# A bidirectional selective scan: four of sixteen states injected by a diagonal matmul, conv outputs on ScalarE

## The chip, the cores and the metric

One NeuronCore of one Trainium2 chip runs the whole kernel in one launch. The metric is the device time of an execution in microseconds, the median of several. The work is fp32 in the part that is changed.

## The reference, cut to what matters

The network is a Mamba-like block (two directions) followed by an attention and mixture-of-experts block, with layer norms between. The change is in the first block, on a batch of 2 sequences of 2,048 tokens, 512 inner channels and 16 states:

```
xc = silu(causal_conv(x_in, conv_w) + conv_b)
dt, B, C = split(xc @ xp_w.T);  dt = softplus(dt @ dt_w.T + dt_b)
for t:  h = exp(dt_t * A) * h + (dt_t * x_t) * B_t     # for 512 channels x 16 states
        y_t = sum over states(h * C_t) + D * x_t
```

It is done once forward and once on the flipped sequence. In the rest of this text x in dt*x is xc.

## The kernel before, in words

The function scan_channels does the scan stage. Channels lie on the 128 partitions, in four groups m = 0 to 3 (DT). Time is cut into chunks of 512 steps. A unit f is one chunk of one direction of one batch; there are 2 x 4 x 2 = 16 units, forward and backward in turn (d = 0, 1). A unit has 64 scans, j = 4n + m for state n and channel group m. Each engine runs a list written out by hand, and semaphores join the lists.

For each scan j:

- ScalarE makes dA = exp(dt * A) for state n and group m (`decay`, L564). For each state it also scales the rows of the turned dt*x, where time lies on partitions, by B of that state (`spread_b`, L569): four activations of 128x512 into one of three dBxT buffers.
- TensorE turns the scaled rows back, four 128x128 transposes into one of three PSUM banks (`inject`, L820). It may fill a bank once the scan three back is done. It also adds the products of eight scans earlier into acc by transposes (`add`, L831). In a transpose the data and an identity are the two operands.
- VectorE runs the recurrence over 512 steps (`scan`, L728) from dA, the bank and the saved state, into hh.
- GpSimd copies the last column of hh to the saved state once per state (L514) and multiplies hh by C (L516). hh, hC and dA have two buffers, so scan n needs GpSimd's copy and products of n-2, and `decay` for n waits for the scan of n-2.

Among these stands the front of a coming unit. For unit f+1: `proj` (TensorE, before injects 7 to 10), `proj_out` (ScalarE), `turn_bc` before inject 15, `bt_out` (ScalarE, L538), `dt_of` (TensorE, L792, before injects 18, 21, 24, 27), each followed by `relu` (VectorE, L700, after that scan) and `dt_out` (ScalarE, L546), then one exponential over 2,048 columns (ScalarE, L551), an addition on GpSimd (L493), `softplus_low`, `softplus` and `times_x` (VectorE, L676, L682, L687, after states 8, 9, 10), `front_one_plus` and `front_log` (ScalarE, L556, L560), and four `turn_dtx` with `turned_out` (before inject 49, 51, 53, 55). For unit f+2: `conv` (TensorE, L769, four matmuls of 512 columns before injects 29, 33, 38, 43), each followed by `conv_out`, which adds the bias and copies to xc (VectorE, L694, after that scan), and a SiLU over all of xc (L526). `skip` (L838) multiplies xc by a diagonal of D, in four plain 128x128 matmuls, after injects 14, 16, 19 and 22.

All front results go through a single PSUM bank, fr: TensorE counts fr_mm as it fills it, the engine that empties it counts fr_out, and each filling waits for the emptying before. TensorE's instructions run in order, so an inject written behind a front matmul waits with it.

ScalarE's list in iteration n is: `spread_b(n+1)`, `middle(n)`, four `decay(n+1)`, `tail(n)`. middle(7) is the exponential, middle(8) `front_one_plus`, middle(9) `front_log`; tail(6) is dt_out(3), tail(12) the SiLU.

Of the kernel before, what the change touches and what calls it, by code (L numbers as in the profile page):

```python
# [16 lines left out]
ACT = mybir.ActivationFunctionType  # L17
# [7 lines left out]
P = 128  # L25
# [4 lines left out]
NS = 16  # L30
# [321 lines left out]
def scan_channels(nc, k, xin, crows, y, convw, convb, xpw, dtw, dtb, alog, dskip):  # L352

    with Stage(nc, "scan") as s:
# [5 lines left out]
        cb = s.sb("cb", [P, 2, DT])  # L360
# [21 lines left out]
        fr = s.ps("fr", [P, C])  # L382
# [19 lines left out]
        AT_DT, AT_NEXT, AT_TURN, AT_SKIP = (18, 21, 24, 27), (29, 33, 38, 43), (49, 51, 53, 55), (14, 16, 19, 22)  # L402

        LOOP = 2 * NC

        def bank(l, j):
            return (l * SUB + j) % (LOOP * SUB) % 3

        def turned_slot(l, n):
            return (l * NS + n) % (LOOP * NS) % 3  # L410

# [110 lines left out]
        def _(act):  # L522
# [25 lines left out]
            def front_exp(f, group):  # L548

                act.wait_ge(fr_out, group + 1)  # L550
                act.activation(ee[:, :, :], ee[:, :, :], ACT.Exp, scale=-1.0).then_inc(e_ok, 1)  # L551

            def front_one_plus(f):
                act.wait_ge(e_ok, f + 1)
                act.wait_ge(y_stored, f * 16 + 16)
                act.activation(uu[:, :, :], ee[:, :, :], ACT.Identity, bias=k["one"][:, :]).then_inc(u_ok, 1)  # L556
# [9 lines left out]

            def spread_b(d, l, n):
                for j in range(JT):
                    last = act.activation(dBxT[turned_slot(l, n)][:, j, :], dtxT[d][:, j, :], ACT.Copy,  # L569
                                          scale=bt[d][:, j, NS + n:NS + n + 1])  # L570
                last.then_inc(bd_ok, 1)
# [30 lines left out]
            def unit(b, c, d, f):  # L602
                o, g, first = 1 - d, f + 1, f * FR_ALL + FR_BEGIN

                def middle(n):
                    if n == 2:
                        for half in range(2):
                            evacuate(f, half)
                    if n == 3:
                        proj_out(g, first + FR_PROJ)  # L610
                    if n == 4:
                        bt_out(o, first + FR_BT)
                    if n in (5, 6):
                        dt_out(o, g, n - 4, first + FR_DT + n - 4)
                    if n == 7:
                        front_exp(g, first + FR_DT + 3)
                    if n == 8:
                        front_one_plus(g)
                    if n == 9:
                        front_log(g)  # L620

                def tail(n):
                    if n == 3:
                        store(f)
                    if n == 4:
                        dt_out(o, g, 0, first + FR_DT)
                    if n == 6:
                        dt_out(o, g, 3, first + FR_DT + 3)
                    if n == 12:
                        silu(d, f + 2, first + FR_NEXT + 3)  # L630

                for n in range(NS):
                    q = f * NS + n
                    dn, at = (d, n + 1) if n + 1 < NS else (o, 0)
                    if n + 1 == NS:
                        act.wait_ge(fr_out, first + FR_TURN + JT)
                    act.wait_ge(bx_mm, f * SUB + turned_free(2 * c + d, n + 1))
                    spread_b(dn, (2 * c + d) + (n + 1) // NS, at)
                    middle(n)
                    if n + 1 == NS:  # L640
                        act.wait_ge(dt_ok, g + 1)
                    for m in range(DT):
                        decay(dn, q + 1, at, m)
                    tail(n)
# [8 lines left out]
        def _(dve):  # L653
# [35 lines left out]
            def conv_out(d, f, m, group):  # L689
                if m == 0 and not (isinstance(f, int) and f < 2):  # L690
                    dve.wait_ge(skip_ok, f - 1)
                    dve.wait_ge(front_ok, f - 1)
                dve.wait_ge(fr_mm, group + 1)
                dve.tensor_scalar(xc[d][:, m, :], fr[:, :], cb[:, d, m:m + 1], None, ALU.add).then_inc(fr_out, 1)  # L694
# [36 lines left out]
            def unit(b, c, d, f):  # L731
                o, g = 1 - d, f + 1
                first = f * FR_ALL + FR_BEGIN
                dve.wait_ge(zeroed, b + 1)
                for n in range(NS):
                    for m in range(DT):
                        scan(d, 2 * c + d, f, n, m)
                        at = n * DT + m
                        if at in AT_DT:
                            i = AT_DT.index(at)  # L740
                            relu(o, g, i, first + FR_DT + i)
                        if at in AT_NEXT:
                            i = AT_NEXT.index(at)
                            conv_out(d, f + 2, i, first + FR_NEXT + i)
                        if at in AT_TURN:
                            i = AT_TURN.index(at)
                            turned_out(o, i, first + FR_TURN + i)
                    if n == 8:
                        softplus_low(o, g)
                    if n == 9:  # L750
                        softplus(o, g)
                    if n == 10:
                        times_x(o, g)
# [4 lines left out]
        def _(pe):  # L758
# [52 lines left out]
            for m in range(DT):  # L811
                conv(1, 14 + m, 1, m)

            def inject(l, f, j):
                n, m = j // DT, j % DT
                if m == 0:
                    pe.wait_ge(bd_ok, f * NS + n + 1)
                pe.wait_ge(h_ok, f * SUB + bank_free(l, j))
                for t in range(JT):
                    last = pe.transpose(bx[bank(l, j)][:, t * P:(t + 1) * P],  # L820
                                        dBxT[turned_slot(l, n)][:, t, m * P:(m + 1) * P],
                                        k["ident"][:, :])
                last.then_inc(bx_mm, 1)

            def add(f, a):
# [22 lines left out]
            def unit(b, c, d, f):  # L848
                o, g, first = 1 - d, f + 1, f * FR_ALL + FR_BEGIN
                for j in range(SUB):  # L850
                    if 7 <= j < 11:
                        proj(o, g, first + FR_PROJ, [j - 7])
                    if j == 15:
                        turn_bc(first + FR_BT)
                    if j in AT_DT:
                        m = AT_DT.index(j)
                        dt_of(o, m, first + FR_DT + m)
                    if j in AT_NEXT:
                        m = AT_NEXT.index(j)
                        conv(d, first + FR_NEXT + m, f + 2, m)  # L860
                    if j in AT_TURN:
                        t = AT_TURN.index(j)
                        turn_dtx(g, t, first + FR_TURN + t)
                    inject(2 * c + d, f, j)
                    for a in adds.get(j, []):
                        add(f, a)
                    if j in AT_SKIP:
                        skip(d, AT_SKIP.index(j))
# [1495 lines left out]
```

## Time and profile before

| what | value |
|---|---|
| median of 3 runs | 4084.34 us (4078.41 to 4086.13) |
| profiled execution | 4088.92 us |
| its span | 4087.3 us |
| TensorE busy | 3407.1 us, 83% |
| VectorE busy | 2777.7 us, 68% |
| ScalarE busy | 2461.5 us, 60% |
| GpSimd busy | 1913.2 us, 47% |
| 1,024 scans (L728) | 1243.5 us, 1263 ns each |
| 1,028 scaled-row activations (L569) | 655.4 us |
| 4,096 injecting transposes (L820) | 668.9 us |
| 72 conv_outs (L694) | 52.3 us |

The scan stage lasts from about 200 to 1,872 us of the span; the stages after it are not touched by the change. A busy time of TensorE counts pipelined matmuls, so a duration of one instruction is longer than the distance to the next start; the distance is the rate. The names PE, DVE, ACT and POOL in rows are TensorE, VectorE, ScalarE and GpSimd.

### The profile page before, as it was taken

The page shows a single profiled execution, that of the slowest core. Times are in us where ns is not written, and L with a number is a line of the kernel's source. Part 1 is how long each engine was busy: PE and PEld are TensorE (multiplying, and loading weights), DVE is VectorE, ACT ScalarE, POOL GpSimd, SP SyncE. Part 2 cuts the span into 40 slices and gives each one's busy share as a digit, 9 for nine tenths or more (in the row PEclk, how much of TensorE's full clock was granted, in tenths as well). Part 3 has the DMA queues.
Part 4 walks back from the last instruction along what each step waited for, and adds up shares of the span by engine and source line. Part 5 has one row for each costly group of instructions (what it writes and reads, how often), then busy time and mean ns, then how long its engine had stood idle before and what let it go on. Part 6 is the DMA issues. An engine that isn't in the chain of part 4 may idle for free. (4 is left out here: it accounts for less than half of the span.)

```text
span 4087.3 us, 69747 instructions
## 1 busy us (share of the span) xinstructions
PE 3407.1 (83%) x22940; PEld 2105.2 (52%) x22940; DVE 2777.7 (68%) x4397; ACT 2461.5 (60%) x3860; POOL 1913.2 (47%) x1734
## 2 busy tenths in 40 slices
PE   7568888888888888885876999999999996499994
PEld 3246666666666666664553333333333334366663
DVE  3259999999899999995764777777777753511113
ACT  3259999999999999993220555555555563122111
POOL 1049999999899999995431000000010002512222
PEclk9779999999999999998995999999999997599997
DMA  5633333333333333335634011011011014333323
GB/s 187 187 89 97 97 99 97 95 94 96 93 96 101 96 94 94 94 94 203 221 119 124 9 20 17 9 20 20 7 20 20 7 48 132 129 81 84 86 53 93
DMA packets 162170, 349.72 MB, mean 86 GB/s; under 512 B 20963, under 2 KB 74198, under 8 KB 147344
## 3 DMA queue, kind: packets, MB, share of 16 engines
q1 hardware_dynamic: 129904, 270.96, 23.9%
q0 software_dynamic: 20624, 43.82, 4.2%
q10 hardware_dynamic: 11280, 30.41, 2.0%
q8 instruction: 191, 3.13, 0.3%
q14 instruction: 171, 1.40, 0.1%
HBM read 245.04 MB, written 102.59 MB: 85 GB/s over the span
## 5 line engine op out<-in xcount | busy, mean ns | idle before, releaser
L516 POOL TENSOR_TENSOR scan_hC<-scan_hh,scan_cbc 128x512 f32<-128x512 f32 x1024 | 1376.4, 1374 | 84.5 <-DVE scan_hh L728 76.8
L728 DVE TENSOR_TENSOR_SCAN scan_hh<-scan_dA,scan_state,scan_bx 128x512 f32<-128x512 f32 x1024 | 1243.5, 1263 | 140.9 <-PE scan_bx L820 63.7
L1572 PE MATMUL attend_s<-attend_kt,attend_qt 32*128 32x512 f32 (+3 forms) x2560 | 803.3, 616 | 34.4 <-DMA attend_qt<-attend_zero 27.8
L820 PE MATMUL scan_bx<-kept_ident,scan_dBxT 128*128 128x128 f32 x4096 | 668.9, 289 | 151.0 <-DVE scan_hh L728 121.9
L564 ACT ACTIVATE scan_dA<-scan_dt,scan_an 128x512 f32<-128x512 f32 x1028 | 661.4, 712 | 30.5 <-DVE scan_hh L728 30.5
L820 PEld LDWEIGHTS scan_bx<-kept_ident,scan_dBxT 128*128 128x128 f32 x4096 | 487.7, 147 | 358.8 <-DVE scan_hh L728 243.2
L831 PE MATMUL scan_acc<-kept_ident,scan_hC 128*128 128x128 f32 x4128 | 646.4, 283 | 29.6 <-POOL scan_hC L516 22.6
L1593 PE MATMUL attend_s<-attend_qt,attend_kt 32*128 32x512 f32 (+3 forms) x2560 | 643.6, 588 | 16.3 <-POOL attend_pb L1449 13.9
L569 ACT ACTIVATE scan_dBxT<-scan_dtxT,scan_bt 128x512 f32<-128x512 f32 x1028 | 655.4, 711 | 0.2
L1483 DVE TENSOR_REDUCE attend_mx<-attend_s 128x1 f32<-128x512 f32 x768 | 494.9, 686 | 203.1 <-PE attend_s L1572 202.0
L1543 ACT ACTIVATE attend_pb<-attend_s 128x1024 f32<-128x1024 f32 x384 | 390.8, 1024 | 285.9 <-PE attend_s L1593 285.9
L1449 POOL TENSOR_SCALAR_AFFINE_SELECT attend_pb<-attend_pb 128x512 f32<-128x512 f32 x128 | 81.3, 636 | 990.6 <-ACT attend_pb L1552 990.6
L831 PEld LDWEIGHTS scan_acc<-kept_ident,scan_hC 128*128 128x128 f32 x4128 | 509.3, 148 | 43.5 <-POOL scan_hC L516 35.5
L1613 PE MATMUL attend_pv<-attend_pb,attend_vall 128*32 128x256 f32 (+1 forms) x4608 | 360.3, 388 | 31.7 <-POOL attend_pb L1449 30.8
L1572 PEld LDWEIGHTS attend_s<-attend_kt,attend_qt 32*128 32x128 f32 x2560 | 302.2, 196 | 118.8 <-DVE attend_mx L1483 44.2
L1593 PEld LDWEIGHTS attend_s<-attend_qt,attend_kt 32*128 32x128 f32 x2560 | 201.7, 189 | 261.6 <-issue 209.0
L1613 PEld LDWEIGHTS attend_pv<-attend_pb,attend_vall 128*32 128x32 f32 x4608 | 94.9, 109 | 416.2 <-issue 311.2
L2160 ACT ACTIVATE experts_hid<-experts_ph,weights_b1t 128x512 f32<-128x512 f32 x128 | 87.9, 687 | 335.8 <-PE experts_ph L2186 335.8
L2098 POOL DMA_INDIRECT scratch_x<-experts_yt,experts_idx x64 | 99.6, 1556 | 380.9 <-DVE experts_yt L2131 375.9
L1546 ACT ACTIVATE attend_below<-attend_s 128x256 f32<-128x256 f32 x256 | 98.3, 384 | 254.1 <-PE attend_s L1593 250.0
L1487 DVE TENSOR_REDUCE attend_mx<-attend_s 128x1 f32<-128x256 f32 (+2 forms) x384 | 160.7, 419 | 108.8 <-PE attend_s L1572 108.6
L2186 PE MATMUL experts_ph<-experts_xT,weights_w1t 128*128 128x512 f32 x512 | 223.2, 596 | 1.3 <-DVE experts_xT L2113 0.9
(208 smaller groups left out, 3838.1 us busy)
## 6 DMA issues: line engine op xcount, KB each, us to landing
scan_xs<-scratch_xin SPq DMA_DIRECT2D x288, 256.0 KB, 6.2
scan_cbc<-scratch_crows SPq DMA_DIRECT2D x64, 1024.0 KB, 4.8
scratch_y<-scan_uu ACTq DMA_DIRECT2D x17, 1024.0 KB, 5.7
scratch_exp_in<-proj_cleared SPq DMA_DIRECT2D x8, 1044.0 KB, 8.4
experts_xt<-scratch_exp_in SPq DMA_DIRECT2D x8, 1044.0 KB, 5.2
scratch_xin<-proj_out_x SPq DMA_DIRECT2D x8, 1024.0 KB, 5.9
scratch_sz<-proj_out_z SPq DMA_DIRECT2D x8, 1024.0 KB, 6.3
mix_yf<-scratch_y SPq DMA_DIRECT2D x8, 1024.0 KB, 6.6
```

The costliest lines, as they stand in the source:

```text
L516: pool.tensor_tensor(hC[n % 2][:, m, :], h[:, m, :], rows, ALU.mult).then_inc(hc_ok, 1)
L564: act.activation(dA[n % 2][:, m, :], dt[d][:, m, :], ACT.Exp, scale=an[:, d, m, n:n + 1]).then_inc(da_ok, 1)
L569: last = act.activation(dBxT[turned_slot(l, n)][:, j, :], dtxT[d][:, j, :], ACT.Copy, scale=bt[d][:, j, NS + n:NS + n + 1])
L728: dve.tensor_tensor_scan(hh[n % 2][:, m, r], dA[n % 2][:, m, r], bx[bank(l, j)][:, r], state[:, d, n, m:m + 1], ALU.mult, ALU.add).then_in ...
L820: last = pe.transpose(bx[bank(l, j)][:, t * P:(t + 1) * P], dBxT[turned_slot(l, n)][:, t, m * P:(m + 1) * P], k["ident"][:, :])
L831: last = pe.matmul(acc[:, j, m * P:(m + 1) * P], hC[n % 2][:, m, j * P:(j + 1) * P], k["ident"][:, :], start=a == 0, stop=False, is_transp ...
L1483: dve.tensor_reduce(mx[:, h, t, c:c + 1], bank[:, :], AX_X, ALU.max).then_inc(s1_read, 1)
L1543: act.activation(own, score[:, :, :], ACT.Exp).then_inc(exp_ok, 1)
L1572: pe.matmul(s1[v % S1][:, 0:w], qt[n % SETS][rows, t * P:(t + 1) * P], kt_[n % SETS][rows, c * C:c * C + w], start=True, stop=True).then_i ...
L1593: last = pe.matmul(s2[pair][:, i, o:], kt_[n % SETS][rows, kt * P:(kt + 1) * P], qt[n % SETS][rows, qc * C + o:(qc + 1) * C], start=True, ...
L1613: last = pe.matmul(pv[32 * h:32 * h + 32, lo:hi], vall[:, b * KT + kt, g * HG + h, :], pb[at % PB][:, h, lo:hi], start=kt == 0 and half == ...
L2186: last = pe.matmul(ph[q % 2][:, :], w1t[e % 2][:, m, f * P:(f + 1) * P], xT[:, m, ch * C:(ch + 1) * C], start=m == 0, stop=m == KD - 1)
```

## The change

For states 2, 6, 10 and 14, ScalarE no longer scales four tiles of 128x512. It scales the 128x128 identity by B, once for each of the four time tiles, which gives four diagonal matrices in the first 128 columns of the dBxT buffer. TensorE's inject then multiplies the turned dt*x (stationary) by that diagonal (moving), in four plain fp32 matmuls, where it transposed scaled rows. The other twelve states stay as they were. In the loop, conv_out goes from VectorE (after scans 29, 33, 38, 43) to ScalarE: for m = 0, 1, 2 at the head of middle(8), middle(9), middle(10), and for m = 3 in tail(11). TensorE's conv stays at its places. The conv_outs before the loop stay on VectorE.

```diff
--- before.py
+++ after.py
@@ -402,6 +402,7 @@
         AT_DT, AT_NEXT, AT_TURN, AT_SKIP = (18, 21, 24, 27), (29, 33, 38, 43), (49, 51, 53, 55), (14, 16, 19, 22)
 
         LOOP = 2 * NC
+        DIAGONAL = (2, 6, 10, 14)
 
         def bank(l, j):
             return (l * SUB + j) % (LOOP * SUB) % 3
@@ -550,6 +551,13 @@
                 act.wait_ge(fr_out, group + 1)
                 act.activation(ee[:, :, :], ee[:, :, :], ACT.Exp, scale=-1.0).then_inc(e_ok, 1)
 
+            def conv_out(d, f, m, group):
+                if m == 0:
+                    act.wait_ge(skip_ok, f - 1)
+                    act.wait_ge(front_ok, f - 1)
+                act.wait_ge(fr_mm, group + 1)
+                act.activation(xc[d][:, m, :], fr[:, :], ACT.Identity, bias=cb[:, d, m:m + 1]).then_inc(fr_out, 1)
+
             def front_one_plus(f):
                 act.wait_ge(e_ok, f + 1)
                 act.wait_ge(y_stored, f * 16 + 16)
@@ -566,6 +574,10 @@
 
             def spread_b(d, l, n):
                 for j in range(JT):
+                    if n in DIAGONAL:
+                        last = act.activation(dBxT[turned_slot(l, n)][:, j, 0:P], k["ident"][:, :], ACT.Copy,
+                                              scale=bt[d][:, j, NS + n:NS + n + 1])
+                        continue
                     last = act.activation(dBxT[turned_slot(l, n)][:, j, :], dtxT[d][:, j, :], ACT.Copy,
                                           scale=bt[d][:, j, NS + n:NS + n + 1])
                 last.then_inc(bd_ok, 1)
@@ -603,6 +615,8 @@
                 o, g, first = 1 - d, f + 1, f * FR_ALL + FR_BEGIN
 
                 def middle(n):
+                    if n in (8, 9, 10):
+                        conv_out(d, f + 2, n - 8, first + FR_NEXT + n - 8)
                     if n == 2:
                         for half in range(2):
                             evacuate(f, half)
@@ -620,6 +634,8 @@
                         front_log(g)
 
                 def tail(n):
+                    if n == 11:
+                        conv_out(d, f + 2, 3, first + FR_NEXT + 3)
                     if n == 3:
                         store(f)
                     if n == 4:
@@ -739,9 +755,6 @@
                         if at in AT_DT:
                             i = AT_DT.index(at)
                             relu(o, g, i, first + FR_DT + i)
-                        if at in AT_NEXT:
-                            i = AT_NEXT.index(at)
-                            conv_out(d, f + 2, i, first + FR_NEXT + i)
                         if at in AT_TURN:
                             i = AT_TURN.index(at)
                             turned_out(o, i, first + FR_TURN + i)
@@ -811,15 +824,18 @@
             for m in range(DT):
                 conv(1, 14 + m, 1, m)
 
-            def inject(l, f, j):
+            def inject(d, l, f, j):
                 n, m = j // DT, j % DT
                 if m == 0:
                     pe.wait_ge(bd_ok, f * NS + n + 1)
                 pe.wait_ge(h_ok, f * SUB + bank_free(l, j))
                 for t in range(JT):
-                    last = pe.transpose(bx[bank(l, j)][:, t * P:(t + 1) * P],
-                                        dBxT[turned_slot(l, n)][:, t, m * P:(m + 1) * P],
-                                        k["ident"][:, :])
+                    if n in DIAGONAL:
+                        last = pe.matmul(bx[bank(l, j)][:, t * P:(t + 1) * P], dtxT[d][:, t, m * P:(m + 1) * P],
+                                         dBxT[turned_slot(l, n)][:, t, 0:P], start=True, stop=True)
+                    else:
+                        last = pe.transpose(bx[bank(l, j)][:, t * P:(t + 1) * P],
+                                            dBxT[turned_slot(l, n)][:, t, m * P:(m + 1) * P], k["ident"][:, :])
                 last.then_inc(bx_mm, 1)
 
             def add(f, a):
@@ -861,7 +877,7 @@
                     if j in AT_TURN:
                         t = AT_TURN.index(j)
                         turn_dtx(g, t, first + FR_TURN + t)
-                    inject(2 * c + d, f, j)
+                    inject(d, 2 * c + d, f, j)
                     for a in adds.get(j, []):
                         add(f, a)
                     if j in AT_SKIP:
```

## Rows read from the trace of the kernel before

**Rows 1.** Busy us of each engine in two stretches (us, busy, records; clock, DMA).
```profile
900.00:1000.00 100.00, 84.33 (x613) 68.45 (x612) 91.79 (x79) 93.74 (x143) 92.21 (x82) 0.95 0.36 96
945.00:984.00 39.00, 36.22 (x280) 30.38 (x278) 37.90 (x35) 38.99 (x64) 38.56 (x40) 1.00 0.48 136
```

**Rows 2.** ScalarE in order of time: start, duration (us), line, operation.
```profile
902.79 0.69 ACT L546 ACTIVATE scan_ee<-scan_fr,scan_db 128x512 f32<-128x512 f32 x1 [1.39 <-DVE scan_dt L700]
903.38 2.55 ACT L569 ACTIVATE scan_dBxT<-scan_dtxT,scan_bt 128x512 f32<-128x512 f32 x4
905.83 1.90 ACT L551 ACTIVATE scan_ee<-scan_ee 128x2048 f32<-128x2048 f32 x1
907.63 2.54 ACT L564 ACTIVATE scan_dA<-scan_dt,scan_an 128x512 f32<-128x512 f32 x4
...
912.53 1.99 ACT L556 ACTIVATE scan_uu<-scan_ee,kept_one 128x2048 f32<-128x2048 f32 x1
...
984.30 0.25 ACT L538 ACTIVATE scan_bt<-scan_fr 128x128 f32<-128x128 f32 x1
```

**Rows 3.** TensorE in order of time.
```profile
903.53 1.07 PE L769 MATMUL scan_fr<-scan_xs,scan_taps 128*32 128x512 f32 x8 [1.51 <-ACT scan_ee L546]
...
908.17 1.06 PE L769 MATMUL scan_fr<-scan_xs,scan_taps 128*32 128x512 f32 x8
...
936.45 1.11 PE L820 MATMUL scan_bx<-kept_ident,scan_dBxT 128*128 128x128 f32 x4 [2.91 <-DVE scan_hh L728]
...
968.28 1.02 PE L778 MATMUL scan_fr<-scan_xc,scan_wp 128*96 128x512 f32 x2
...
981.85 1.06 PE L838 MATMUL scan_acc<-scan_ddiag,scan_xc 128*128 128x128 f32 x8
982.75 0.60 PE L820 MATMUL scan_bx<-kept_ident,scan_dBxT 128*128 128x128 f32 x4
983.18 0.60 PE L831 MATMUL scan_acc<-kept_ident,scan_hC 128*128 128x128 f32 x4
984.60 1.12 PE L792 MATMUL scan_fr<-scan_pr,scan_wrk 64*128 64x512 f32 x2 [0.82 <-ACT scan_bt L538]
```

**Rows 4.** VectorE in order of time.
```profile
900.83 1.28 DVE L728 TENSOR_TENSOR_SCAN scan_hh<-scan_dA,scan_state,scan_bx 128x512 f32<-128x512 f32 x1 [0.91 <-PE scan_bx L820]
...
905.31 1.28 DVE L728 TENSOR_TENSOR_SCAN scan_hh<-scan_dA,scan_state,scan_bx 128x512 f32<-128x512 f32 x1 [1.36 <-PE scan_bx L820]
906.50 0.73 DVE L694 TENSOR_SCALAR scan_xc<-scan_fr,scan_cb 128x512 f32<-128x512 f32 x1
907.14 4.79 DVE L728 TENSOR_TENSOR_SCAN scan_hh<-scan_dA,scan_state,scan_bx 128x512 f32<-128x512 f32 x4
...
914.85 2.27 DVE L676 SCALAR_TENSOR_TENSOR scan_ee<-scan_uu,scan_dt 128x2048 f32<-128x2048 f32 x1
918.50 3.62 DVE L728 TENSOR_TENSOR_SCAN scan_hh<-scan_dA,scan_state,scan_bx 128x512 f32<-128x512 f32 x3 [1.39 <-POOL scan_state L514]
...
953.14 27.04 DVE L728 TENSOR_TENSOR_SCAN scan_hh<-scan_dA,scan_state,scan_bx 128x512 f32<-128x512 f32 x23
...
986.43 1.28 DVE L728 TENSOR_TENSOR_SCAN scan_hh<-scan_dA,scan_state,scan_bx 128x512 f32<-128x512 f32 x1 [1.68 <-ACT scan_dA L564]
```

**Rows 5.** GpSimd's addition, in two units.
```profile
807.44 4.59 POOL L493 TENSOR_TENSOR scan_dt<-scan_dt,scan_ee 128x2048 f32<-128x2048 f32 x1 [4.11 <-ACT scan_ee L551]
...
907.80 4.58 POOL L493 TENSOR_TENSOR scan_dt<-scan_dt,scan_ee 128x2048 f32<-128x2048 f32 x1 [4.11 <-ACT scan_ee L551]
```

**Rows 6.** Groups by line and shape: records, busy us, mean ns, idle before.
```profile
L820 PE MATMUL scan_bx<-kept_ident,scan_dBxT 128*128 128x128 f32 x4096 | 668.9, 289 | 151.0 <-DVE scan_hh L728 121.9 <-ACT scan_dBxT L569 19.7
...
L838 PE MATMUL scan_acc<-scan_ddiag,scan_xc 128*128 128x128 f32 x512 | 67.6, 275 | 0.0
```

**Rows 7.** Busy us and granted clock, two stretches.
```profile
936.00:938.00 2.00, 1.55 (x8) 1.55 (x9) 2.00 (x3) 1.12 (x2) 2.00 (x4) 0.50 0.00 0
953.00:968.00 15.00, 13.91 (x106) 11.15 (x105) 15.00 (x14) 15.00 (x26) 14.66 (x14) 1.00 0.16 53
```

## The prediction

> **What bounds the kernel now.** I read the busy time by stretch first, then one period of the scan, engine by engine in order of time. The scan stage has 16 units at a period of 100.35 us (807.44 to 907.80 from one unit's addition on GpSimd to the next [rows 5]). Four engines are nearly full: in 100 us ScalarE is busy 93.7, GpSimd 92.2, VectorE 91.8, TensorE 84.3 [rows 1]. None of them alone is the bound, so shares decide little; the period is a loop through all four. I number the 64 scans of a unit j = 4n+m.
>
> 1. Scan 27 at 900.83 is followed by relu(3). ScalarE then runs dt_out(3) at 902.79, spread_b(8), the exponential, decay(8), and spread_b(9) until 912.53, without a gap [rows 2]. TensorE's conv(0), before inject 29, waits for dt_out(3): it starts at 903.53, and scan 29 at 905.31 [rows 3, 4].
> 2. GpSimd waits 4.11 us for that exponential and adds until 912.35, and scan 36 waits 1.39 us for its copy of the state, until 918.50 [rows 4, 5].
> 3. VectorE goes on with scans and front work and starts scan 56 at 953.14; call this T. From T it scans 23 times in a row, 1.172 us each [rows 4].
> 4. In the next unit TensorE squeezes proj between the injects. From 968.28 it has no gap to 983.62; dt_of(0) waits for bt_out and starts at 984.60 [rows 3], and scan 18 starts at 986.43 = T + 33.3 [rows 4]. Scan 27 of this unit comes 14.75 us later (one period after 900.83), and the loop is closed.
>
> **The change part by part.**
>
> *ScalarE.* A full spread is four activations in 2.45 us (903.38 to 905.83 [rows 2]), 0.61 each. No row has this operation on 128 columns from SBUF with a scale. Bounds: 0.25 (the whole duration of bt_out, 128 columns, no scale [rows 2]) and 0.61 (nothing saved). I take 0.29, nearer to the short one: 2,048 columns take 1.80 (905.83 to 907.63 [rows 2]), which allows at most 0.83 ns a column plus 0.1; 512 columns at that slope leave 0.19 fixed, and 128 add 0.11. So 16 x 0.32 = 5.1 us a unit go. Four conv_outs at 0.59 (902.79 to 903.38, same shape and source [rows 2]) come: 2.4. Net -2.7. VectorE loses four of 0.64 (906.50 to 907.14 [rows 4]): -2.6. GpSimd keeps its work.
>
> *TensorE.* An inject is four transposes, 0.43 start to start (982.75 to 983.18 [rows 3]). Its replacement is four plain fp32 matmuls, and the trace has those in skip, 128x128 each: 0.90 for four (981.85 to 982.75 [rows 3]), with 8 records. The means hide this, 275 and 289 ns a record, but skip has 512 records for its 256 matmuls and inject 4,096 for its 4,096 transposes [rows 6]: a plain fp32 matmul counts twice. So each of the 16 diagonal injects of a unit costs 0.46 more, 7.4 us on an engine with about 15 to spare. Bounds: 0 (the diagonal runs as a transpose does) and 0.9 (all at the half clock, where an inject takes 0.9 for 0.44). It matters where they lie:
>  - n=2 (j 8 to 11) lies in the gapless stretch of point 4: +1.84, less the pause of 0.98 before dt_of(0) (983.62 to 984.60). Scan 18 comes at T + 34.1, +0.8.
>  - n=6 (j 24 to 27): inject 24's delay is lost in a wait of dt_out(2) for ScalarE's own list. Inject 27 directly follows dt_out(2) and dt_of(3), so relu(3) is +0.4.
>  - n=10, n=14: TensorE is up to three banks ahead, and VectorE's 3 us operations give it time. Inject and add take 1.34 against 1.17 a scan, so four in a row use 0.7 of that lead. At half clock they would take 2.7; I put 0.2 a unit.
>
> *conv_out on ScalarE*, the largest term. On VectorE conv_out(0) came right after scan 29, at 906.50, so conv(1) could start at 908.17 [rows 3, 4]. Now it heads middle(8), behind the exponential, decay(8) and spread_b(9), none of them shortened: 912.53, counted from relu(3). conv(1) stands on TensorE's list ahead of inject 33 and waits for it; queued behind it are inject 33 and the adds, and scan 33 waits for those. conv_out(0) ends at 913.22; at full clock scan 33 follows 1.78 after conv(1) starts (as 903.53 to 905.31 [rows 3, 4]), at 915.05. VectorE without its conv_outs would be free for it at 910.05. That is a stall of 5.0 us. But TensorE then idles from 908.2 to 913.3, and after a pause of 2.91 us the granted clock stood at 0.50, its 1.2 GHz level, and an inject took 0.9 [rows 3, 7]. So I expect conv(1) and inject 33 at that level: scan 33 near 916.3, the end of scan 35 near 920.3, softplus_low (2.27 [rows 4]) to 922.5, scan 36 at 922.5 for 918.50: +4.0. The wait of 1.39 for GpSimd is swallowed in this. conv_out(2) and (3) then leave 1.3 on VectorE: T comes 2.7 late. Bounds: +1.0 (the clock never falls) and +4.2 (low until scan 36). The later conv_outs hold nothing up: conv_out(1) runs near 918.7, and conv(2) at j=38 is not reached before 921.
>
> *What the savings buy.* After T ScalarE is ahead by two diagonal spreads (n=14, n=2), 2.6 us; decay(2), which waits for scan 67, lets 1.9 of it through, so bt_out would come at T + 29.3 for T + 31.2. But TensorE is now the later one (T + 32.3), so none of it reaches scan 18. Around relu ScalarE waits for VectorE (1.39 at 902.79 [rows 2]); a shorter spread_b(6) only lengthens that.
>
> *A rule weighed.* From 953 to 968 TensorE runs transposes alone, and its granted clock is 1.00, 2.4 GHz [rows 7]. The Trainium skill, "TensorE: Matmul & The Clock Gate", section "Part 4: PE-mode transpose", says that a transpose does not count as busy for the clock and so does not bring the full rate. By that rule, plain matmuls would raise a clock that transposes leave low; the trace disagrees.
>
> **Sum.** 2.7 + 0.8 + 0.4 + 0.2 = 4.1 us a unit, x 16 = 66 us. The profiled execution took 4088.92 (span 4087.3), so 4155 for one like it. It lies 4.6 above the median of the three, 4084.34; on the median, 4150.
>
> **The rivals.**
>  - *ScalarE is the bound* (faster). For: 93.7%; busy without a gap from 945 to 984 [rows 1]; GpSimd waits 4.11 for its exponential. Then its net 2.7 x 16 = 43 is won: 4041. This decides if conv_out(0) is done before TensorE comes to conv(1), at 908.2, 5 us earlier than its list allows. Against: that list is gapless and holds no diagonal spread there. 0.10.
>  - *The clock holds* over the gap before conv(1): 1.0 + 0.8 + 0.4 + 0.1 = 2.3, x 16 = 37: 4121. Against: a shorter pause dropped it. 0.12.
>  - *Plain matmuls lift the clock* so far that the diagonal states cost no more than now: 2.7 x 16 = 43: 4127. For: clock below 1 in parts of the period; against: full clock under transposes [rows 7]. 0.03. This is where the page's rule would lead.
>  - *Low clock spreads* from the stall to scan 36: 4.2 + 1.4 = 5.6, x 16 = 90: 4174. 0.12.
>  - *The diagonal matmuls hide* wholly, and ScalarE's lead is worth its 1.9: 2.7 - 1.9 = 0.8, x 16 = 13: 4097. Against: the 8 records. 0.08.
>  - *Stall and savings cancel* (clock holds and lead partly kept): 4084. 0.03.
>
> **Numbers.** The forecast has 0.52. A change of under 0.2% (8 us) can't be told from none. Faster: 0.10 and 0.01 of the last, 0.11; same 0.04; slower 0.85. The range runs from the hidden matmuls to just above the low-clock case, 4097 to 4178, and leaves the faster side out.
>
> **What would show it.** L820: 5,120 records for 4,096, four-matmul injects of 0.90. Once a unit a TensorE gap of about 5 us before conv(1), waiting for ScalarE's conv_out, and a clock of 0.50 after it; VectorE waiting some 6 us for TensorE at scan 33, the 1.39 for GpSimd gone. Small spreads near 0.3. A period of 104.4. I am wrong if scan 33 follows scan 32 closely, if the period is under 101, or if bt_out still holds dt_of(0).

## The result: 4138.1 us, 54 us slower than before

The changed kernel takes 4138.13 us (median of 4 runs, 4136.85 to 4142.68) against 4084.20 for the kernel before, run beside it: a ratio of 1.0136, 95% interval 1.0119 to 1.0154. The forecast was 4150 (+66), in a range of 4097 to 4178. The profiled execution has a span of 4135.9 us.

In the tables below a unit is cut at the starts of four scans. The segment 27-36 (from the start of scan 27 to that of scan 36) holds the front's chain on ScalarE and the first convs, 36-56 two of VectorE's long operations, 56-18 the stretch with proj into the next unit, 18-27 the relu hops. All are means in us over the 14 regular units of one profiled execution; the unit across the two batches is left out, as its GpSimd clears the state.

```
                27-36   36-56   56-18   18-27   period
before          17.65   33.98   33.97   14.77   100.4
after           22.36   31.75   34.29   15.22   103.6
difference      +4.71   -2.23   +0.32   +0.45   +3.2      x 16 = 52 us
```

The loss is in 27-36, and 36-56 gives nearly half of it back. VectorE of the changed kernel in order of time; the first row here answers to the scan at 900.83 in [rows 4], so the times of this unit are later by 23.90 us than those in the rows of before:

```profile
924.73 1.28 DVE L744 TENSOR_TENSOR_SCAN scan_hh<-scan_dA,scan_state,scan_bx 128x512 f32<-128x512 f32 x1 [0.91 <-PE scan_bx L834]
...
929.20 4.80 DVE L744 TENSOR_TENSOR_SCAN scan_hh<-scan_dA,scan_state,scan_bx 128x512 f32<-128x512 f32 x4 [1.36 <-PE scan_bx L837]
940.25 3.85 DVE L744 TENSOR_TENSOR_SCAN scan_hh<-scan_dA,scan_state,scan_bx 128x512 f32<-128x512 f32 x3 [6.25 <-ACT scan_dA L572]
944.02 3.17 DVE L692 SCALAR_TENSOR_TENSOR scan_ee<-scan_uu,scan_dt 128x2048 f32<-128x2048 f32 x1
947.12 4.78 DVE L744 TENSOR_TENSOR_SCAN scan_hh<-scan_dA,scan_state,scan_bx 128x512 f32<-128x512 f32 x4
...
978.87 18.88 DVE L744 TENSOR_TENSOR_SCAN scan_hh<-scan_dA,scan_state,scan_bx 128x512 f32<-128x512 f32 x16
```

Scan 29 (929.20) is where it was. Four scans later VectorE waits 6.25 us for scan 33. The profile credits the wait to ScalarE's dA, which had long been made (L572 at 931.52 in ScalarE's rows below); TensorE's list and ScalarE's tell what it was:

```profile
927.42 1.07 PE L782 MATMUL scan_fr<-scan_xs,scan_taps 128*32 128x512 f32 x8 [1.51 <-ACT scan_ee L547]
928.42 0.66 PE L837 MATMUL scan_bx<-kept_ident,scan_dBxT 128*128 128x128 f32 x4
...
931.53 0.60 PE L847 MATMUL scan_acc<-kept_ident,scan_hC 128*128 128x128 f32 x4
937.14 1.93 PE L782 MATMUL scan_fr<-scan_xs,scan_taps 128*32 128x512 f32 x8 [5.01 <-ACT scan_xc L559]
939.01 1.11 PE L837 MATMUL scan_bx<-kept_ident,scan_dBxT 128*128 128x128 f32 x4
```

ScalarE in the same stretch:

```profile
926.69 0.69 ACT L547 ACTIVATE scan_ee<-scan_fr,scan_db 128x512 f32<-128x512 f32 x1 [1.89 <-DVE scan_dt L716]
927.27 2.55 ACT L581 ACTIVATE scan_dBxT<-scan_dtxT,scan_bt 128x512 f32<-128x512 f32 x4
929.72 1.90 ACT L552 ACTIVATE scan_ee<-scan_ee 128x2048 f32<-128x2048 f32 x1
931.52 2.55 ACT L572 ACTIVATE scan_dA<-scan_dt,scan_an 128x512 f32<-128x512 f32 x4
933.97 2.55 ACT L581 ACTIVATE scan_dBxT<-scan_dtxT,scan_bt 128x512 f32<-128x512 f32 x4
936.42 0.67 ACT L559 ACTIVATE scan_xc<-scan_fr,scan_cb 128x512 f32<-128x512 f32 x1
936.99 2.00 ACT L564 ACTIVATE scan_uu<-scan_ee,kept_one 128x2048 f32<-128x2048 f32 x1
```

conv_out(0) is the new line L559 at 936.42, right behind spread_b(9). conv(1), L782, waited 5.01 us for it and took 1.87 us to the next start, where conv(0), at 927.42, took 1.00. Between them the clock fell. Busy us of each engine and TensorE's granted clock, columns as in [rows 1]:

```profile
931.00:937.00 6.00, 1.13 (x11) 0.90 (x9) 3.00 (x3) 6.00 (x11) 5.30 (x2) 0.77 0.64 135
937.00:940.00 3.00, 2.85 (x13) 1.20 (x14) 0.00 (x0) 3.00 (x4) 3.00 (x4) 0.50 0.00 0
941.00:947.00 6.00, 5.61 (x48) 4.36 (x47) 5.88 (x4) 6.00 (x11) 6.00 (x5) 0.99 0.97 170
```

The granted clock was 0.77 on the mean of the stretch with the gap and 0.50, the level of 1.2 GHz, from 937 to 940, where TensorE was busy 2.85 of 3 us; VectorE was busy 0.00 in it. In every unit the clock falls in this wait or within 0.3 us behind it. Over the stretch 300 to 1700 the waits say the same (us in total, times, longest us):

```profile
PE scan_fr L782 <- ACT scan_xc L559: 70.2, 14, 5.0
```

The groups answer to [rows 6]. The diagonal injects are 16 x 16 x 4 = 1,024 matmuls and leave 2,048 records; a diagonal activation takes 0.39 us by itself, 0.29 start to start (four from 941.34 to 942.51):

```profile
L837 PE MATMUL scan_bx<-kept_ident,scan_dBxT 128*128 128x128 f32 x3072 | 501.5, 288 | 90.2 <-DVE scan_hh L744 75.0 <-ACT scan_dBxT L581 9.2
...
L834 PE MATMUL scan_bx<-scan_dBxT,scan_dtxT 128*128 128x128 f32 x2048 | 273.8, 278 | 15.4 <-DVE scan_hh L744 15.4
...
L578 ACT ACTIVATE scan_dBxT<-kept_ident,scan_bt 128x128 f32<-128x128 f32 x256 | 81.3, 391 | 0.2
```

### The profile page after: what moved, and what is told of

The parts are those of the page before. It is cut to its first block and busy times, and to the rows that moved or that the text cites. A ratio compares the mean times of both kernels' runs of the same rounds, so it can differ in the third digit from the quotient of the medians.

```text
span 4135.9 us, 71779 instructions
## 1 busy us (share of the span) xinstructions
PE 3474.5 (84%) x23964; PEld 2207.8 (53%) x23964; DVE 2737.3 (66%) x4333; ACT 2423.9 (59%) x3924; POOL 1915.3 (46%) x1734
## 5 line engine op out<-in xcount | busy, mean ns | idle before, releaser
L517 POOL TENSOR_TENSOR scan_hC<-scan_hh,scan_cbc 128x512 f32<-128x512 f32 x1024 | 1285.1, 1279 | 141.9 <-DVE scan_hh L744 116.1
L572 ACT ACTIVATE scan_dA<-scan_dt,scan_an 128x512 f32<-128x512 f32 x1028 | 668.1, 715 | 50.6 <-DVE scan_hh L744 50.4
L847 PE MATMUL scan_acc<-kept_ident,scan_hC 128*128 128x128 f32 x4128 | 630.2, 279 | 1.1 <-POOL scan_hC L517 1.1
L837 PE MATMUL scan_bx<-kept_ident,scan_dBxT 128*128 128x128 f32 x3072 | 501.5, 288 | 90.2 <-DVE scan_hh L744 75.0
L1559 ACT ACTIVATE attend_pb<-attend_s 128x1024 f32<-128x1024 f32 x384 | 390.7, 1024 | 282.6 <-PE attend_s L1609 282.6
L581 ACT ACTIVATE scan_dBxT<-scan_dtxT,scan_bt 128x512 f32<-128x512 f32 x772 | 492.2, 712 | 3.8 <-PE scan_bx L834 3.8
L837 PEld LDWEIGHTS scan_bx<-kept_ident,scan_dBxT 128*128 128x128 f32 x3072 | 368.2, 148 | 216.5 <-DVE scan_hh L744 145.8
L834 PEld LDWEIGHTS scan_bx<-scan_dBxT,scan_dtxT 128*128 128x128 f32 x2048 | 251.1, 192 | 81.8 <-DVE scan_hh L744 43.6
L834 PE MATMUL scan_bx<-scan_dBxT,scan_dtxT 128*128 128x128 f32 x2048 | 273.8, 278 | 15.4 <-DVE scan_hh L744 15.4
```

Source lines behind the costliest of these rows:

```text
L517: pool.tensor_tensor(hC[n % 2][:, m, :], h[:, m, :], rows, ALU.mult).then_inc(hc_ok, 1)
L572: act.activation(dA[n % 2][:, m, :], dt[d][:, m, :], ACT.Exp, scale=an[:, d, m, n:n + 1]).then_inc(da_ok, 1)
L834: last = pe.matmul(bx[bank(l, j)][:, t * P:(t + 1) * P], dtxT[d][:, t, m * P:(m + 1) * P], dBxT[turned_slot(l, n)][:, t, 0:P], start=True, ...
L837: last = pe.transpose(bx[bank(l, j)][:, t * P:(t + 1) * P], dBxT[turned_slot(l, n)][:, t, m * P:(m + 1) * P], k["ident"][:, :])
L847: last = pe.matmul(acc[:, j, m * P:(m + 1) * P], hC[n % 2][:, m, j * P:(j + 1) * P], k["ident"][:, :], start=a == 0, stop=False, is_transp ...
L1559: act.activation(own, score[:, :, :], ACT.Exp).then_inc(exp_ok, 1)
```

## The experiments

Each was timed beside the kernel before on the same chip, and each edit below is against the changed kernel. The column us is the median time, and the ratio is to the kernel before of the same session, whose medians lie between 4084.2 and 4086.5. The segments of all runs:

```
                                       27-36  36-56  56-18  18-27  period   us       ratio (95%)
before                                 17.65  33.98  33.97  14.77  100.4
after                                  22.36  31.75  34.29  15.22  103.6    4138.1   1.0136 (1.0119 to 1.0154)
diagonal states alone (diag_only)      17.67  34.16  34.27  15.22  101.3    4102.5   1.0042 (1.0027 to 1.0057)
conv_out alone (conv_only)             22.36  31.78  34.07  14.78  103.0    4127.2   1.0111 (1.0093 to 1.0129)
after, TensorE kept busy (warm)        20.11  31.45  34.29  15.22  101.1    4102.0   1.0038 (1.0023 to 1.0052)
conv_out alone, kept busy (warm_conv)  20.11  31.42  34.27  14.76  100.6    4090.9   1.0012 (1.0002 to 1.0023)
after, conv_out(0) early (conv0_early) 18.14  31.74  34.29  15.22   99.4    4075.2   0.9980 (0.9971 to 0.9989)
the same, no diagonals (early_nodiag)  18.14  31.94  35.92  14.73  100.7    4091.9   1.0010 (1.0000 to 1.0020)
one diagonal state, n=2 (d2)           17.64  34.02  34.23  14.76  100.7    4094.0   1.0017 (1.0008 to 1.0027)
one diagonal state, n=14 (d14)         17.66  34.02  32.73  14.75   99.1    4068.7   0.9952 (0.9939 to 0.9966)
early, states 0, 9, 11, 14 (early_move)18.12  32.24  32.55  14.74   97.7    4046.4   0.9893 (0.9878 to 0.9908)
early, states 0, 10, 14 (early_three)  18.14  31.75  32.55  14.75   97.2    4040.6   0.9890 (0.9874 to 0.9905)
split, states 0, 10, 14 (split_three)  17.59  31.76  32.53  14.74   96.6    4030.8   0.9864 (0.9848 to 0.9880)
```

### The two halves of the change, each alone

The diagonal states alone, conv_out back on VectorE:

```diff
-                    if n in (8, 9, 10):
-                        conv_out(d, f + 2, n - 8, first + FR_NEXT + n - 8)
...
+                        if at in AT_NEXT:
+                            i = AT_NEXT.index(at)
+                            conv_out(d, f + 2, i, first + FR_NEXT + i)
```

> The four diagonal states as in the changed kernel, conv_out back on VectorE after scans 29, 33, 38, 43. Theory (two causes: the late place of conv_out(0) on ScalarE's list, and the doubled TensorE records of states 2 and 6): the stall before scan 33 is gone, T (scan 56) lies where it was before, 52.3 us after relu(3) less or plus 0.3, scan 18 comes at T + 34.3 and scan 27 15.2 later. Period 100.35 + 1.0 + 0.5 = 101.8, so +23 us: 4107. Rival (TensorE's added load as a whole is the price, wherever it lies, 7.4 us a unit on the fullest engine): all of the +54 stays, 4138. Rival (ScalarE's savings pass through once conv_out is off it): below 4084.

Measured 4102.5, +17 by the ratio against the +23 expected. The stall is gone (27-36 17.67) and 18-27 is 15.22, as said. From scan 36 to scan 18 it grew by 0.5 and not 1.0. The rival of TensorE's total load, 4138, is out, and so is the one under 4084.

conv_out alone:

```diff
-        DIAGONAL = (2, 6, 10, 14)
+        DIAGONAL = ()
```

> No diagonal states, conv_out on ScalarE as in the changed kernel. Theory: a stall of about 6 us at scan 33 with a TensorE gap of 5 us before conv(1) and a clock of 0.50 behind it, T +1.8 against before; T to scan 18 stays 33.3 or grows a little, since ScalarE has lost nothing there and is 1.8 us no later relative to T; period about 102.2, so +30 us: 4114. The two parts then add up to the change (23 + 30 = 53 against 54 measured). Rival (TensorE's load is the price): within 5 us of 4084. Rival (the parts hide each other): both alone cost nearly the whole.

Measured 4127.2, +45 by the ratio of 1.0111, where +30 was expected: the larger part by far. Its 27-36 is the changed kernel's. I had priced the rest against the one unit that I read, and that was not a typical one: T comes 54.1 us after scan 27, 1.8 more than in that unit, as expected, but 56-18 is 34.07 on the mean and not 33.3. By the ratios the parts add to 62 us, for 54 of the whole.

### Is it the clock or the waiting?

Before conv(1), TensorE turns 40 tiles into the bank that inject 33 then overwrites:

```diff
+                    if j == AT_NEXT[1]:
+                        pe.wait_ge(h_ok, f * SUB + bank_free(2 * c + d, j))
+                        for t in range(40):
+                            pe.transpose(bx[bank(2 * c + d, j)][:, (t % JT) * P:(t % JT + 1) * P],
+                                         dBxT[turned_slot(2 * c + d, j // DT)][:, t % JT, 0:P], k["ident"][:, :])
```

> The changed kernel, with 40 added transposes on TensorE before conv(1), into the bank that inject 33 then overwrites, so that TensorE is busy in the 5 us it waits for conv_out(0). They take 40 x 0.11 = 4.4 us and end at about 912.9 on the clock of the unit of before, just before conv_out(0) ends. Theory (the low clock after the gap makes conv(1) and inject 33 slow, 1.3 us): scan 33 comes 1.3 us earlier, 13.0 us after relu(3) begins where it now comes 14.3 after; T 0.5 to 1.3 earlier; period 102.3 to 103.0, 4138 less 8 to 21 us: 4117 to 4130. Rival (the clock is beside the point, the waiting for ScalarE is all): no change from 4138, or slower by what the added work delays.

Measured 4102.0: 36 us came back by the medians, 40 by the ratios, more than the 8 to 21 expected, by work whose results nobody reads. TensorE and VectorE of that run:

```profile
916.19 4.53 PE L877 MATMUL scan_bx<-kept_ident,scan_dBxT 128*128 128x128 f32 x40
921.37 1.07 PE L782 MATMUL scan_fr<-scan_xs,scan_taps 128*32 128x512 f32 x8 [0.65 <-ACT scan_xc L559]
922.36 0.66 PE L837 MATMUL scan_bx<-kept_ident,scan_dBxT 128*128 128x128 f32 x4
```

```profile
908.94 1.28 DVE L744 TENSOR_TENSOR_SCAN scan_hh<-scan_dA,scan_state,scan_bx 128x512 f32<-128x512 f32 x1 [0.91 <-PE scan_bx L834]
...
923.14 3.62 DVE L744 TENSOR_TENSOR_SCAN scan_hh<-scan_dA,scan_state,scan_bx 128x512 f32<-128x512 f32 x3 [4.93 <-PE scan_bx L837]
926.68 2.28 DVE L692 SCALAR_TENSOR_TENSOR scan_ee<-scan_uu,scan_dt 128x2048 f32<-128x2048 f32 x1
928.89 4.78 DVE L744 TENSOR_TENSOR_SCAN scan_hh<-scan_dA,scan_state,scan_bx 128x512 f32<-128x512 f32 x4
```

Its busy times and clock in two stretches of that wait, columns as in [rows 1]:

```profile
916.00:920.00 4.00, 4.00 (x39) 4.00 (x38) 2.21 (x2) 4.00 (x7) 4.00 (x1) 1.00 0.73 159
920.00:926.00 6.00, 5.35 (x48) 4.28 (x47) 2.85 (x3) 6.00 (x10) 6.00 (x7) 1.00 0.37 65
```

The clock stays at 1.00, conv(1) takes 0.99 to the next start and scan 33 comes 14.20 us after scan 27 (908.94 to 923.14), where it came 15.52 after (924.73 to 940.25). That is the 1.3 expected. No regular unit of this run has the clock at its lower level between scans 27 and 36. Another 0.2 in this unit, 0.3 on the mean, is in scans 34 and 35, which no longer follow slow injects (3.54 from scan 33 to softplus_low for 3.77). The remainder I had not counted. softplus_low takes 2.28 and not 3.17, and GpSimd's rows tell why. In the changed kernel:

```profile
939.87 0.18 POOL L515 COPY scan_state<-scan_hh 128x4 f32<-128x4 f32 x1
940.01 4.99 POOL L517 TENSOR_TENSOR scan_hC<-scan_hh,scan_cbc 128x512 f32<-128x512 f32 x4
944.95 2.30 POOL L515 COPY scan_state<-scan_hh 128x4 f32<-128x4 f32 x1
947.21 2.62 POOL L517 TENSOR_TENSOR scan_hC<-scan_hh,scan_cbc 128x512 f32<-128x512 f32 x2
```

With the clock kept up:

```profile
924.30 7.04 POOL L517 TENSOR_TENSOR scan_hC<-scan_hh,scan_cbc 128x512 f32<-128x512 f32 x4
```

In both, GpSimd multiplies without a pause of its own, a product about every 1.24 us. softplus_low starts in the midst of one and ends 2.15 to 2.2 us after that product does: 947.19 after 945.00 in the changed kernel, 928.96 after 926.81 here, where it is the second of the four products. Meanwhile GpSimd's next instruction waits (the copy of 2.30 us, the four products of 7.04). So in the changed kernel it is GpSimd's product that sets scan 36: scan 35 starts anywhere from 17.89 to 18.87 us after scan 27, softplus_low takes from 3.43 down to 2.37, and scan 36 comes 22.34 to 22.42 after scan 27 in every unit. With the clock kept up softplus_low comes in two products earlier in 12 of the 14 units, and scan 36 comes at 19.92 to 19.95; in the other two it just misses that product, and scan 36 comes at 21.17. So the low clock cost 1.3 us at scan 33 and, rounded up to whole products, 2.4 at scan 36 in most units.

The same added transposes with no diagonal states:

> No diagonal states, conv_out late on ScalarE, and the 40 added transposes before conv(1). Theory (the low clock after the gap is the price of the late conv_out, whatever the diagonal states do): 27 to 36 falls by 2.3 us as in the run with diagonal states (22.3 to 20.1), so 4127 less 16 x 2.2: 4092 (4084 to 4100). So at full clock the late conv_out costs only about 5 us, since VectorE is freed of 2.6 us a unit. Rival (the clock matters only with TensorE's doubled states behind the stall): no more than 10 us under 4127.

Measured 4090.9, 36 us under conv_out alone (40 by the ratios). So at the full clock the late conv_out costs some 5 us: its longer 27-36 (20.11 for 17.65) is nearly paid by the shorter 36-56 (31.42 for 33.98), where VectorE is freed of two conv_outs and its softplus and times_x take less. The low clock, with what it brings about on GpSimd, is the price of the move, with or without diagonal states.

### Is it the place?

```diff
-                    if n in (8, 9, 10):
-                        conv_out(d, f + 2, n - 8, first + FR_NEXT + n - 8)
+                    if n in (7, 8, 10):
+                        m = (7, 8, 10).index(n)
+                        conv_out(d, f + 2, m, first + FR_NEXT + m)
```

> The changed kernel, with conv_out(0) at the head of middle(7), ahead of the exponential, and conv_out(1) at the head of middle(8); conv_out(2) and (3) where they are. Theory: conv_out(0) is done about 3 us after relu(3), before TensorE comes to conv(1), so the stall before scan 33 goes; the exponential and GpSimd's addition come 0.6 later. T at +0.6 - 1.3 = -0.7 against before, scan 18 at T + 34.3, scan 27 15.2 later: period 100.35 - 0.7 + 1.0 + 0.5 = 101.15, +13 us: 4097. Rival (ScalarE's load from conv_out is the price, not its place): stays near 4138.

Measured 4075.2, 63 us under the changed kernel. The edit moves conv_out(0) ahead of the exponential, and conv_out(1) into the place that it leaves. It is 0.2% under before, where +13 was expected. The stall is gone. 36-56 fell by 2.2 where I counted 1.3, and 56-18 grew by 0.3 where I counted 1.0: together 1.6 of the 1.8 us a unit by which I was off.

The same without diagonal states:

> No diagonal states; conv_out on ScalarE with conv_out(0) ahead of the exponential and conv_out(1) at the head of middle(8). Theory: scan 27 to 36 as in the run with both (18.1), 36 to 18 as in the run of conv_out alone (66.0), 18 to 27 14.72: period 98.9, 16 x 1.7 below before: 4086 - 27 = 4059, 16 us under the same with diagonal states (4075). So the diagonal states are a loss in their places even when conv_out is mended. Rival (the gain of the early conv_out rests on what the diagonal states save on ScalarE): 4075 or more.

My theory failed here, and its rival (4075 or more) held: 4091.9, not 4059. 56-18 grew to 35.92. Scan 12, in the midst of that segment, starts at 984.18 (the credit to dA is again wrong). The rows are VectorE's, TensorE's and ScalarE's:

```profile
958.26 23.53 DVE L745 TENSOR_TENSOR_SCAN scan_hh<-scan_dA,scan_state,scan_bx 128x512 f32<-128x512 f32 x20
984.18 1.28 DVE L745 TENSOR_TENSOR_SCAN scan_hh<-scan_dA,scan_state,scan_bx 128x512 f32<-128x512 f32 x1 [2.39 <-ACT scan_dA L572]
986.37 2.59 DVE L745 TENSOR_TENSOR_SCAN scan_hh<-scan_dA,scan_state,scan_bx 128x512 f32<-128x512 f32 x2 [0.91 <-PE scan_bx L838]
```

```profile
978.59 1.04 PE L838 MATMUL scan_bx<-kept_ident,scan_dBxT 128*128 128x128 f32 x8
981.74 1.36 PE L848 MATMUL scan_acc<-kept_ident,scan_hC 128*128 128x128 f32 x8 [2.11 <-ACT scan_uu L590]
```

```profile
979.78 1.90 ACT L590 ACTIVATE scan_uu<-scan_acc 128x1024 f32<-128x1024 f32 x2
```

VectorE scans 20 times in a row and waits 2.39 us; TensorE, ahead of inject 12, had waited 2.11 us with its add (L848) for ScalarE to empty acc (L590, started at 979.78). ScalarE has no gap from 957 to 994 here. Behind this wait the clock fell again:

```profile
983.00:985.00 2.00, 2.00 (x11) 2.00 (x10) 0.82 (x1) 2.00 (x4) 2.00 (x3) 0.50 1.00 166
```

That happens in 8 of the 14 units, and 56-18 is 36.4 in these; in the other six, at full clock, it is 35.0 to 35.7, 35.3 on the mean. So of the 1.95 us that it grew about 1.3 is the wait for ScalarE and the rest the clock. Once the stall is mended ScalarE is the bound there, with the four conv_outs (2.4 us a unit) on it and nothing taken off. That the longer stall had let it catch up in the run of conv_out alone is how I read it; no run shows it by itself. So conv_outs and diagonal states belong together after all: at the same early place the states save 12 us by the ratios, 17 by the medians, though they cost 0.5 a unit in the relu hops.

### Which diagonal states pay?

Two runs have conv_out on VectorE, as before, and a single diagonal state. The first:

```diff
-        DIAGONAL = (2, 6, 10, 14)
+        DIAGONAL = (2,)
```

> conv_out on VectorE, one diagonal state only, n=2, which lies in TensorE's stretch with proj. Theory: TensorE's extra 1.84 us there moves it to be the last at scan 18 and swallows what ScalarE saves (1.28): scan 36 to scan 18 stays 67.95 in the units without low clock and grows by up to 0.9 in the others; scan 18 to 27 stays 14.72. Mean period +0.0 to +0.4: 4086 to 4092. Rival (ScalarE's saving passes through): -1.3 a unit, 4066. Rival (TensorE's 1.84 adds in full): 4115.

> conv_out on VectorE, one diagonal state only, n=14, where TensorE has slack after VectorE's copies of the turned dtx. Theory: between the SiLU and bt_out ScalarE has no gap and sets scan 18, so a saving of 1.28 us in spread_b(14) passes through: scan 36 to 18 falls from 67.95 to about 66.7, all else unchanged; period 99.1 for 100.35: 4086 - 20 = 4066. Rival (a diagonal state costs TensorE's 1.84 us wherever it lies): same or slower than before. Rival (the saving goes into a wait of decay for the scans): same.

With n=2 alone 4094.0 was measured, 2 us above the stretch that I gave. 56-18 is 34.22 to 34.24 in every regular unit, whatever the clock did before T, as it would be if TensorE's gapless stretch alone set it; in the kernel before it varies from 33.3 to 34.3. With `DIAGONAL = (14,)` 4068.7 was measured, 4066 expected: 56-18 is 32.73, 1.2 shorter. By the ratios one state in one place loses 7 us, in another it gains 20.

With conv_out(0) early, `DIAGONAL = (0, 9, 11, 14)`:

> Early conv_out(0) as above, and four diagonal states at n = 0, 9, 11, 14 in place of 2, 6, 10, 14. Theory: no diagonal inject lies beside proj (n=2) or behind dt_of (n=6), and two saved spreads (14, 0) lie between the SiLU and bt_out: of 2.56 us about 1.9 reaches scan 18, TensorE's lag from n=0 costs up to 0.7. Scan 36 to 18 about 64.1 to 64.8, 18 to 27 14.72, 27 to 36 18.1: period 97.0 to 97.7, 4086 - 16 x 3 = 4038 (4028 to 4048), below both kernels. Rival (TensorE's total load is the price): 4075 or more.

And `DIAGONAL = (0, 10, 14)`:

> Early conv_out(0), diagonal states n = 0, 10, 14. Theory: as early_move, without the states 9 and 11, whose injects lie between scans 36 and 56 (32.2 there for 31.7 in the run with 2, 6, 10, 14) : 27 to 36 18.1, 36 to 56 31.7, 56 to 18 32.5, 18 to 27 14.7: period 97.1, half a microsecond a unit under early_move: 4038. Rival (each state saved on ScalarE still counts, as the run without any showed): 4046 or more.

Measured 4046.4 (4028 to 4048 expected) and 4040.6 (4038 expected). The segment 36-56 went from 32.24 to 31.75 between them, as expected; the ratios (0.9893 and 0.9890) do not part the two runs by themselves. Last, with the same three states, conv_out(0) stays on VectorE after scan 29, the other three go to ScalarE:

```diff
-                    if n in (8, 9, 10):
-                        conv_out(d, f + 2, n - 8, first + FR_NEXT + n - 8)
+                    if n in (8, 10):
+                        m = (0, 8, 10).index(n)
+                        conv_out(d, f + 2, m, first + FR_NEXT + m)
...
+                        if at == AT_NEXT[0]:
+                            conv_out(d, f + 2, 0, first + FR_NEXT)
```

> Diagonal states n = 0, 10, 14; conv_out(0) on VectorE after scan 29, conv_out(1) at the head of middle(8), (2) and (3) as in the changed kernel. Theory: the exponential is not put off by 0.6 and VectorE has 1.4 us to spare before scan 36, so 27 to 36 is 17.7 again, the rest as early_three: period 96.7, 8 us under early_three: 4030. Rival (VectorE's 0.64 comes off a stretch that it bounds): the same as early_three.

4030.8 us, 1.4% under before and 107 us under the changed kernel, with edits of the same two kinds at other places: three diagonal states for four, and three conv_outs on ScalarE for four. VectorE of this run:

```profile
927.95 27.14 DVE L745 TENSOR_TENSOR_SCAN scan_hh<-scan_dA,scan_state,scan_bx 128x512 f32<-128x512 f32 x23
956.11 3.62 DVE L745 TENSOR_TENSOR_SCAN scan_hh<-scan_dA,scan_state,scan_bx 128x512 f32<-128x512 f32 x3 [1.03 <-POOL scan_hC L517]
960.47 1.28 DVE L745 TENSOR_TENSOR_SCAN scan_hh<-scan_dA,scan_state,scan_bx 128x512 f32<-128x512 f32 x1 [0.74 <-PE scan_bx L840]
...
975.20 1.28 DVE L745 TENSOR_TENSOR_SCAN scan_hh<-scan_dA,scan_state,scan_bx 128x512 f32<-128x512 f32 x1 [0.91 <-PE scan_bx L840]
...
979.67 1.28 DVE L745 TENSOR_TENSOR_SCAN scan_hh<-scan_dA,scan_state,scan_bx 128x512 f32<-128x512 f32 x1 [1.36 <-PE scan_bx L840]
980.87 0.73 DVE L711 TENSOR_SCALAR scan_xc<-scan_fr,scan_cb 128x512 f32<-128x512 f32 x1
981.51 7.13 DVE L745 TENSOR_TENSOR_SCAN scan_hh<-scan_dA,scan_state,scan_bx 128x512 f32<-128x512 f32 x6
989.49 3.13 DVE L693 SCALAR_TENSOR_TENSOR scan_ee<-scan_uu,scan_dt 128x2048 f32<-128x2048 f32 x1 [0.85 <-ACT scan_uu L564]
992.79 4.79 DVE L745 TENSOR_TENSOR_SCAN scan_hh<-scan_dA,scan_state,scan_bx 128x512 f32<-128x512 f32 x4 [0.18 <-POOL scan_state L515]
```

Scan 18 (960.47) comes 32.52 after scan 56 (927.95), and scan 36 (992.79) 17.59 after scan 27 (975.20). conv_out(0), at 980.87, has its 0.64 us in a stretch that otherwise waited.

## Why the prediction came out right, and where its sizes were off

- **The stall at scan 33**, the largest term: right in place, cause and size. Scan 33 was to come 15.5 after scan 27 (900.83 to 916.3); it came 15.52 after. The gap of 5.1 us was 5.01, and the clock behind it 0.50. The two runs with TensorE kept busy show what the clock was worth: 36 to 40 us of 54. The prediction gave it 1.8 us a unit (4.1 in the sum, 2.3 in the rival where the clock holds), 29 us; the rest it cost through GpSimd's products, which the prediction did not have.
- **27-36 in all**: +4.0 expected, +4.7 measured. Scans 33 to 35 took 3.77 for the 4.0 that I gave them, and softplus_low, taken at its old 2.27, now takes 3.17 (at 944.02; before at 914.85, [rows 4]). The path from scan 33 through softplus_low to scan 36 was so not quite the true one: I had GpSimd's part "swallowed", but the product that softplus_low waits for sets scan 36, wherever between 17.89 and 18.87 us after scan 27 scan 35 starts. That the sum came near with this part missing is in part luck.
- **36-56**: -1.3 expected, -2.2 measured. This is the term whose size was furthest off. In most units of the changed kernel softplus and times_x take 2.62 each, for 2.97 and 3.08 before, as each comes in later on a product of GpSimd: 0.8 that I had not counted. The shortest units of the two kernels, 33.65 and 31.52, differ by 2.1, which is two conv_outs and these 0.8.
- **56-18**: +0.8 expected, +0.3 measured. Here a single unit was taken for all. In the unit that I read, scan 49 waited 0.88 us for a TensorE at low clock, so 36-56 took 34.64 and 56-18 only 33.3; the 14 regular units give 33.98 and 33.97, and in many no such wait stands. (Its 18-27 was 15.13 too, and not the 14.75 that I worked out.) The mechanism held. TensorE sets scan 18 at T + 34.3 (34.1 expected), and d2 shows that it swallows ScalarE's saving there, while d14 shows the saving where TensorE is not last.
- **18-27**: +0.4 expected, +0.45 measured, in every run with n=6 diagonal and in none without. The doubled records were right: 5,120 for 4,096.
- **0.2 for low clock in the diagonal states** was not seen in the changed kernel: its 36-56 is 31.75, and 31.78 without them. With conv_out on VectorE they add 0.2 there (34.16 for 33.98). Sum: 4.1 expected, 3.2 measured, x 16: 66 and 52. The terms that were too small and too large partly cancel.
- **The rule of the Trainium skill** ("TensorE: Matmul & The Clock Gate", section "Part 4: PE-mode transpose"), that a transpose does not count as busy for the clock: the runs with 40 added transposes disagree. The clock stayed at 1.00 over 4.5 us of them, in place of falling.
- **The rival "ScalarE is the bound"** was wrong for this kernel and right one edit further, as the run without diagonal states and with an early conv_out(0) shows.

## What to carry to other kernels

Moving an operation to another engine changes its time less than its turn: look what stands ahead of it on the new list, and what stands behind its consumer on that engine's list. A wait of some 5 us on TensorE was paid twice here, as a wait and as a low clock after it. A term read from one unit of a loop belongs beside the same term of the others: here one unit gave 33.3 us for a segment of 34.0 on the mean. When several engines are nearly full, place each added cost by segment of the loop: one diagonal state lost 7 us at one place and won 20 at another.

## What the runs showed of the hardware that was not expected

- Forty transposes that nobody needs, 4.5 us a unit, made two kernels 36 us faster each (40 by the ratios), by holding TensorE's clock at 1.00 through a wait.
- When a VectorE operation with two inputs over 2,048 columns meets GpSimd, the one that started first goes on and the other waits for it. In the changed kernel softplus_low, softplus and times_x start 48 times in the midst of a product of GpSimd. The product keeps its 1.27 to 1.31 us in all 48, and the VectorE operation ends 2.15 to 2.21 us after it, so that it takes 2.37 to 3.43 in all. The GpSimd instruction behind ends with it: a copy of four columns took 2.30 us beside softplus_low's 3.17 (944.95, above), and 0.18 at 939.87. Where softplus_low started with a product, at 914.85 in the kernel before, it kept its 2.27, and three products took 5.89 us in place of 3.73.
